# Products that nobody reads, issued on TensorE in five waits of a four-stage transformer kernel

## The chip, the cores and the metric

The kernel runs on one core of one Trainium2 chip. The metric is the device time of one execution in microseconds (us). TensorE is called PE, its weight loads PEld, VectorE DVE, ScalarE ACT, GpSimd POOL and SyncE SP, as in the rows of the profile.

## The reference

Two transformer layers over 2 x 1024 tokens of width 128, each an attention and a mixture of eight experts, each behind a layer norm and with a residual:

```python
x = x + _L0_attn_ref(_layernorm(x), ...)   # delta-rule attention, 4 heads, five branches, gates, fused, @ o_w
x = x + _L0_ffn_ref(_layernorm(x), ...)    # 8 experts, top 2, silu(x @ gate) * (x @ up) @ down
x = x + _L1_attn_ref(_layernorm(x), ...)   # 16 heads of width 8, rotary, softmax over 1024 keys, @ Wo + bo
x = x + _L1_ffn_ref(_layernorm(x), ...)    # 8 experts, top 1, gelu, @ Wo, layer norm
```

The end of the first attention, which the change touches, is

```python
fused = fused * jax.lax.rsqrt(jnp.mean(fused * fused, -1, keepdims=True) + 1e-05) * onorm_w
return fused.reshape(B, L, H * dv) @ o_w
```

## The kernel before

The 2048 tokens are 16 tiles of 128 (`NT`) in four blocks of 512 (`NB`). The four stages (`attn0`, `ffn0`, `attn1`, `ffn1`) run one behind the other, with `nc.all_engine_barrier()` between them (lines 2550 and 2557 are the first two). Each stage is one hand-written instruction stream for each engine; semaphores order them. At a barrier each engine has to have finished its own stream before any of them goes on.

The end of `attn0` on PE: for each block `j`, `mean_square(j)` (line 2390) sums the squares over the heads into a PSUM bank, ACT takes the root in two activations (lines 2097 and 2100, with a table load between them), DVE scales (line 1825), and `out(j)` (line 2397) multiplies by `o_w`. DVE adds that to `x` (line 1832) and takes the statistics of the next norm (lines 117 and 120). Some products of this stage are already ones that nobody reads: `hold(bank, times)`, line 2386, each 128 x 512 in bf16.

The head of `ffn0` and of `attn1`: DVE makes the roots (lines 127 and 129) and then 16 normalized tiles (`norm_rows`, line 135). PE turns them, four tiles a block (`norm_pe`, line 146), ACT copies each block to `xnT` (line 157). In `ffn0` PE then makes the router's logits (line 191), which DVE waits for at line 229, the first step of the routing. In `attn1` PE turns two blocks and then makes the projections of queries and keys, two products a block (lines 877 and 878), which DVE takes at lines 998 and 1000.

The end of `ffn0`: the expert loop ends on PE; ACT scales the rows that came back by DMA (line 612), and after each block increments `f0_scaled`, eight times in all (`2 * NB`). DVE adds and takes statistics.

Of the kernel before, what the change touches and what calls it, by code (L numbers as in the profile page):

```python
# [6 lines left out]
BF16 = mybir.dt.bfloat16  # L7
# [4 lines left out]
P = 128  # L12
# [4 lines left out]
BLK = 512  # L17
NB = T // BLK
# [120 lines left out]
def norm_pe(c, banks, blocks=range(NB)):  # L139
    pe, ps, k, xn, ident = c.pe, c.psum, c.turn, c.mem["xn"], c.mem["ident"]  # L140
    for b in blocks:
        pe.wait_ge(c.sem("n_row"), NT * k + TPB * (b + 1))
        if b >= len(banks):
            pe.wait_ge(c.sem("n_xnt"), NB * k + b - len(banks) + 1)
        for j in range(TPB):
            mm = pe.transpose(ps[:, banks[b % len(banks)], j * P:(j + 1) * P], xn[:, TPB * b + j, :], ident[:])
        mm.then_inc(c.sem("n_turned"), 1)
# [35 lines left out]
def logits_pe(c, name, weights):  # L183


    pe, ps, S = c.pe, c.psum, c.sem
    tokens = c.mem["xnT"][:, 0:T].rearrange("p (t q i) -> p t q i", q=4, i=32)
    for n in range(NB):
        pe.wait_ge(S("n_xnt"), NB * c.turn + n + 1)
        for q in range(4):  # L190
            mm = pe.matmul(ps[32 * q:32 * q + 32, 2, n * P:(n + 1) * P], weights, tokens[:, n * TPB:(n + 1) * TPB, q, :],
                           start=True, stop=True, skip_group_check=True)
    mm.then_inc(S(name + "_lgt"), 1)


def route_pe(c, name, top):
    pe, ps, s, S = c.pe, c.psum, c.mem, c.sem
    n, TC = width_of(top), top * NT
    pe.wait_ge(S(name + "_chosen"), 1)
    pe.wait_ge(c.own_pool.sem, c.filled)  # L200
    chosen = s["sel" if top == 2 else "first"][:].rearrange("p t e -> p (t e)")
    pe.matmul(ps[:, 3, 0:NT * NE], s["earlier"][:], chosen, start=True, stop=True)
    pe.matmul(ps[:, 4, 0:NT * NE], s["ones"][:], chosen, start=True, stop=True).then_inc(S(name + "_counted"), 1)
    step = 2 * TPB
    for q in range(0, TC, step):
        pe.wait_ge(S(name + "_lane"), q // step + 1)
        pe.wait_ge(S(name + "_carry"), q // step + 1)
        for k in range(q, q + step):
            mm = pe.matmul(ps[:, 5, 0:2 * n], s["at_lane"][:, k, :], s["carry"][:, k].rearrange("p c n -> p (c n)"),
                           start=k == 0, stop=k == TC - 1)  # L210
    mm.then_inc(S(name + "_found"), 1)
# [346 lines left out]
    return lambda b: c.mem["xnT"][:, b * BLK:(b + 1) * BLK]  # L558


def rows_out_sp(c, name, k, rows=NT):

    c.sp.wait_ge(c.sem("n_row"), NT * c.turn + rows)
    c.sp.dma_start(c.rows_x[k].rearrange("(p t) d -> p t d", p=P), c.mem["xn"][:]).then_inc(c.sem(name + "_rows"), 16)


def ffn0_sp(c, w):
    for name in ("up", "down"):
        c.sp.dma_start(c.mem["e_" + name][:], w["f0_" + name]).then_inc(c.sem("f0_weights"), 16)
    c.weights = 32  # L570
    rows_out_sp(c, "f0", 0)
    attn1_loads(c, w)
    results_sp(c, "f0", 2, c.rows_y[0])
# [18 lines left out]


def ffn0_pe(c):
    norm_pe(c, (6, 7))
    c.pe.wait_ge(c.sem("f0_tables"), c.tables)
    logits_pe(c, "f0", c.mem["f0_rw"][:])
    route_pe(c, "f0", 2)
    experts_pe(c, "f0", 2, True)


def ffn0_act(c):
# [14 lines left out]
def ffn0(c, w, x):  # L617
    ffn0_sp(c, w)
    ffn0_dve(c, x)
    ffn0_pe(c)  # L620
    ffn0_act(c)
    route_pool(c, "f0", 2)
    experts_pool(c, "f0", 2, c.rows_x[0], c.rows_y[0])
    attn1_ahead(c)
# [236 lines left out]
def attn1_pe(c):  # L861
    pe, ps, m, S = c.pe, c.psum, c.mem, c.sem
    xnT, q, kk, va, pt, o = m["xnT"], m["a1_q"], m["a1_k"], m["a1_va"], m["a1_p"], m["a1_o"]
    norm_pe(c, NORM_BANKS, (0, 1))
    pe.wait_ge(c.ahead.sem, c.ahead.n)

# [479 lines left out]
def attn1(c, w, x):  # L1346
    attn1_sp(c)
    attn1_pe(c)
    attn1_act(c, x)
    attn1_dve(c, x)  # L1350
    attn1_pool(c, x)
    tables_sp(c, w, "f1", 1)
# [769 lines left out]
def attn0_pe(c):  # L2122
# [108 lines left out]
    for n in range(NB):  # L2231
# [3 lines left out]
        for i, (_, g0, ng) in enumerate(FIRS):  # L2235
# [4 lines left out]
            for g in range(ng):  # L2240
                for h in range(H0):
                    mm = pe.matmul(ps[32 * h:32 * h + 32, fir_bank(n, i), :], m["a0_wfir"][:, (g0 + g) * H0 + h, :],  # L2242
                                   v4[:, h, b, PAD + t0 - 4 * g:PAD + t0 - 4 * g + BLK],
                                   start=g == 0, stop=g == ng - 1, skip_group_check=True)
# [80 lines left out]
    for n in range(NCH):  # L2325
        bank = SUO[n % 2]
        pe.wait_ge(S("a0_wn"), n + 1)
        for b in range(B):
            if n:
                pe.wait_ge(S("a0_sc"), (n - 1) * B + b + 1)  # L2330
            for hs in HEADS:
                mm = pe.matmul(ps[hs, bank[b], 0:3 * CH], st[hs, b, :], sbuf[hs, n % 2, b, :, :],
                               start=False, stop=False, skip_group_check=True)
# [3 lines left out]
        for b in range(B):  # L2337
            pe.wait_ge(S("a0_uh"), n * B + b + 1)
            so = ps[:, bank[b], 0:3 * CH].rearrange("p (o i) -> p o i", o=3)[:, 0:3:2, :]
            for hs in HEADS:  # L2340
                mm = pe.matmul(so[hs], uh[hs, b, :], op[hs, n, b, KTOK:AT + 1, :],
                               start=False, stop=True, skip_group_check=True)
# [45 lines left out]
    def mean_square(j):  # L2388
        pe.wait_ge(S("a0_fu2"), j + 1)
        pe.matmul(ps[:, MS[j], :], m["a0_heads"][:], sq[:, j % 2, :], start=True, stop=True).then_inc(S("a0_ms"), 1)  # L2390

    def out(j):
        pe.wait_ge(S("a0_scaled"), j + 1)
        pe.wait_ge(S("a0_mul"), min(NB * NU - 2 + j, NB * NU))
        for t in range(TPB):
            at = ORD[j] * BLK + t * P
            mm = pe.matmul(ps[:, OUT[j], t * D:(t + 1) * D], fu[:, at:at + P], m["a0_ow"][:], start=True, stop=True)
        mm.then_inc(S("a0_out"), 1)
# [33 lines left out]
    out(0)  # L2432
    mean_square(2)
    out(1)
    mean_square(3)
    out(2)
    out(3)


def attn0(c, w, x):  # L2440
# [144 lines left out]
```

## Time and profile before

| | |
|---|---|
| median of 3 runs | 923.98 us (923.12 to 925.49) |
| the profiled execution | 930.92 us, its span 929.6 us |
| mean granted PE clock | 0.898 |
| PE busy | 756.1 us, 81% of the span |
| DVE busy | 667.4 us, 72% |
| ACT busy | 511.1 us, 55% |

The span runs from the first to the last instruction. The stages lie at about 0 to 238, 238 to 422, 422 to 805 and 805 to 930 us of it. A granted clock of 1.00 is 2.4 GHz, one of 0.50 is 1.2 GHz; a value between them in a window says that the clock changed inside that window.

### The profile page before, as it was taken

Reading aid. Unit: us, or ns where it says so; the run is one execution under the profiler, and the core shown is the slowest. Engines: PE = TensorE matmul, PEld = TensorE weight load, DVE = VectorE, ACT = ScalarE, POOL = GpSimd, SP = SyncE. Lnnn points to the kernel's source line nnn. Section 1 sums busy time; section 2 is a strip of 40 time slices with the busy share of each in tenths; the row PEclk is TensorE's granted clock in tenths of the full one; section 3 lists DMA queues with packets and bytes.
Section 4 is the critical chain, followed back from the end, with each engine's and each line's share of the span. In section 5 each row is a group of like instructions: output and inputs, shape, how many; then the busy total and the mean of one; then the engine's idle time right before and its main releaser. Section 6 shows DMA issues by size and latency. Waiting matters only on the chain. (4 is left out here: it accounts for less than half of the span.)

```text
span 929.6 us, 17693 instructions
## 1 busy us (share of the span) xinstructions
PE 756.1 (81%) x6703; PEld 325.6 (35%) x6704; DVE 667.4 (72%) x1316; ACT 511.1 (55%) x1012; POOL 243.9 (26%) x297
## 2 busy tenths in 40 slices
PE   6999978967329999927887999999999999728880
PEld 2343256633216766714111222222222222215660
DVE  7868964477763344338786999999999998753545
ACT  4744413646203333344346888888888889704343
POOL 0130010323055666460651200000010000025653
PEclk9999979988659999977658999999999999958996
DMA  3520010000731111131876030312300000061113
GB/s 94 119 65 2 1 25 5 4 1 0 269 129 38 43 43 43 35 102 52 233 159 194 2 81 2 81 26 58 80 3 2 3 2 12 1 252 44 43 35 96
DMA packets 40618, 57.62 MB, mean 62 GB/s; under 512 B 12424, under 2 KB 27920, under 8 KB 39768
## 3 DMA queue, kind: packets, MB, share of 16 engines
q1 hardware_dynamic: 36568, 48.36, 19.1%
q0 software_dynamic: 3968, 8.13, 3.1%
q8 instruction: 55, 0.90, 0.4%
q14 instruction: 27, 0.22, 0.1%
HBM read 37.54 MB, written 14.75 MB: 56 GB/s over the span
## 5 line engine op out<-in xcount | busy, mean ns | idle before, releaser
L1019 DVE TENSOR_REDUCE arena<-psum 128x1 f32<-128x1024 f32 x256 | 301.0, 1217 | 23.5 <-PE psum L903 20.7
L1158 ACT ACTIVATE arena<-psum 128x512 f32<-128x512 f32 x512 | 265.9, 605 | 53.7 <-PE psum L922 53.6
L903 PE MATMUL psum<-arena 56*128 56x512 bf16 x512 | 181.0, 413 | 10.7 <-DVE arena L1019 9.1
L922 PE MATMUL psum<-arena 59*128 59x512 bf16 x512 | 156.3, 390 | 5.1 <-ACT arena L1158 3.7
L933 PE MATMUL psum<-arena 128*32 128x512 f32 x1024 | 138.4, 612 | 8.7 <-issue 8.7
L922 PEld LDWEIGHTS psum<-arena 59*128 59x128 bf16 x512 | 38.4, 94 | 165.8 <-ACT arena L1158 142.1
L475 POOL DMA_INDIRECT rows_y<-arena x62 | 61.9, 998 | 61.3 <-DVE arena L426 57.9
L383 PEld LDWEIGHTS psum<-arena 128*128 128x128 f32 x496 | 62.4, 191 | 37.9 <-issue 29.5
L383 PE MATMUL psum<-arena 128*128 (+1 forms) x496 | 66.9, 278 | 9.1 <-ACT arena L454 6.0
L374 PE MATMUL psum<-arena 128*128 x124 | 67.2, 625 | 3.5 <-DVE arena L411 2.7
L1227 POOL TENSOR_SCALAR arena<-arena 128x16 f32<-128x16 f32 x16 | 4.1, 254 | 249.5 <-DVE arena L1019 249.4
L470 POOL DMA_INDIRECT arena<-rows_x,arena x62 | 60.1, 969 | 35.4 <-issue 16.1
L903 PEld LDWEIGHTS psum<-arena 56*128 56x128 bf16 x512 | 37.5, 95 | 71.2 <-DVE arena L1019 69.0
L426 DVE COPY arena<-psum 128x128 f32<-128x128 f32 x62 | 18.1, 291 | 58.2 <-issue 36.3
L454 ACT COPY arena<-psum 128x512 f32<-128x512 f32 x62 | 36.2, 584 | 41.3 <-PE psum L389 37.9
L448 ACT ACTIVATE arena<-psum 128x512 f32<-128x512 f32 x39 | 23.3, 597 | 46.9 <-PE psum L374 46.9
L432 DVE TENSOR_TENSOR arena<-arena,psum 128x512 f32<-128x512 f32 x39 | 26.8, 688 | 23.5 <-PE psum L394 22.0
L2242 PE MATMUL psum<-arena 128*32 128x512 f32 x352 | 41.2, 593 | 0.2 <-DMA arena<-arena 0.2
L394 PE MATMUL psum<-arena 128*128 x78 | 40.8, 606 | 0.0
L389 PE MATMUL psum<-ident,arena 128*128 128x128 f32 x248 | 37.7, 275 | 0.0
L933 PEld LDWEIGHTS psum<-arena 128*32 128x32 f32 x1024 | 20.7, 108 | 42.4 <-issue 38.0
L418 DVE TENSOR_TENSOR arena<-psum,arena 128x512 f32<-128x512 f32 x23 | 15.9, 691 | 25.4 <-PE psum L374 19.5
(319 smaller groups left out, 1110.1 us busy)
## 6 DMA issues: line engine op xcount, KB each, us to landing
arena<-scr_k SPq DMA_DIRECT2D x15, 448.0 KB
arena<-scr_q SPq DMA_DIRECT2D x15, 448.0 KB
arena<-in_f_up SPq DMA_DIRECT2D x1, 4096.0 KB
arena<-rows_y SPq DMA_DIRECT2D x12, 256.0 KB, 4.5
scr_q<-arena SPq DMA_DIRECT2D x6, 384.0 KB, 3.7
arena<-in_f_down SPq DMA_DIRECT2D x1, 2048.0 KB
rows_x<-xn SPq DMA_DIRECT2D x2, 1024.0 KB, 16.8
arena<-in_f_up SPq DMA_DIRECT2D x1, 2048.0 KB, 8.4
```

What stands on the lines that cost most here:

```text
L374: pe.matmul(ps[:, u.pair, :], xt[:, u.pair, :], merged(wup[:, bass.ds(e, 1), 0:F]), start=True, stop=True).then_inc(up, 1)
L383: mm = pe.matmul(ps[:, 5 + 2 * d.pair, 0:P], ht[:, f * P:(f + 1) * P], merged(wdown[:, ed, f * P:(f + 1) * P]), start=f == 0, stop=f == FC ...
L389: mm = pe.transpose(ps[:, 4, f * P:(f + 1) * P], h[:, g.pair, f * P:(f + 1) * P], ident[:])
L394: pe.matmul(ps[:, 2 + u.pair, :], xt[:, u.pair, :], merged(wup[:, bass.ds(e, 1), F:2 * F]), start=True, stop=True).then_inc(again, 1)
L470: pool.indirect_dma_start(xs[:, t % SLOTS, :], None, src, index).then_inc(landed[t % SLOTS], 16)
L475: pool.indirect_dma_start(dst, index, y[:, d.slot, :], None).then_inc(stored[d.slot], 16)
L903: mm = pe.matmul(ps[:, bank + half, :], q[rows, k, h, (qh * 4 + qt) * P:(qh * 4 + qt + 1) * P], kk[rows, k, h, half * BLK:(half + 1) * BLK ...
L922: pe.matmul(ps[:, score_bank(n), :], kk[0:KA, k, h, kb * P:(kb + 1) * P], q[0:KA, k, h, qh * BLK:(qh + 1) * BLK], start=True, stop=True).t ...
L933: mm = pe.matmul(ps[32 * h:32 * h + 32, 7, :], va[:, kb, (st % NG) * HG + h, :], pt[:, (u % 3) * HG + h, :], start=kb == 0, stop=kb == NTB ...
L1019: dve.tensor_reduce(mx[:, qh, h * 4 + qt:h * 4 + qt + 1], ps[:, bank:bank + 2, :].rearrange("p a b -> p (a b)"), X, ALU.max).then_inc(S("a ...
L1158: act.activation(pt[:, (u % 3) * HG + h, :], ps[:, score_bank(n), :], ACT.Exp, scale=float(HD) ** -0.5).then_inc(S("a1_exp"), 1)
L2242: mm = pe.matmul(ps[32 * h:32 * h + 32, fir_bank(n, i), :], m["a0_wfir"][:, (g0 + g) * H0 + h, :], v4[:, h, b, PAD + t0 - 4 * g:PAD + t0 - ...
```

## The change

PE gets 35 more products of 128 x 512 in bf16, whose results nobody reads, at five places: six between `out(1)` and `mean_square(3)`, ten behind `out(3)` at the end of `attn0`, eight at the head of `ffn0` before the first transpose, six behind the expert loop of `ffn0` once ACT has scaled the last rows, five at the head of `attn1`. All but the first six use the identity matrix, read as bf16, and write PSUM bank 0; the first six write bank 1 by the function that stands there already.

```diff
+def idle_products(c, times):
+
+    bits = c.mem["ident"][:].bitcast(BF16)
+    for _ in range(times):
+        c.pe.matmul(c.psum[:, 0, :], bits[:, 0:P], bits[:, 0:1].broadcast_to([P, BLK]), start=True, stop=True)
...
 def ffn0_pe(c):
+    idle_products(c, 8)
     norm_pe(c, (6, 7))
     c.pe.wait_ge(c.sem("f0_tables"), c.tables)
     logits_pe(c, "f0", c.mem["f0_rw"][:])
     route_pe(c, "f0", 2)
     experts_pe(c, "f0", 2, True)
+    c.pe.wait_ge(c.sem("f0_scaled"), 2 * NB)
+    idle_products(c, 6)
...
 def attn1_pe(c):
...
+    idle_products(c, 5)
     norm_pe(c, NORM_BANKS, (0, 1))
...
     mean_square(2)
     out(1)
+    hold(1, 6)
     mean_square(3)
     out(2)
     out(3)
+    idle_products(c, 10)
```

On PE, where `attn0` ends and `ffn0` begins, the order before the change is this (L2397 is `out`, L2390 `mean_square`, L146 the transposes):

```order
L2390 MATMUL psum<-arena 128x512 [waits a0_fu2]
L2397 MATMUL psum<-arena 128x128 [waits a0_mul,a0_scaled]
L2397 MATMUL psum<-arena 128x128 x3
L2397 MATMUL psum<-arena 128x128 [waits a0_mul,a0_scaled]
L2397 MATMUL psum<-arena 128x128 x3
L146 MATMUL psum<-ident,xn 128x128 [waits barrier_Pool_Activation_PE_DVE_SP_release,n_row]
```

With the change the same place on PE reads as follows (L2397 is now the product of `hold`, L2401 `mean_square`, L2408 `out`, L565 the product of `idle_products`):

```order
L2397 MATMUL psum<-arena 128x512 x6
L2401 MATMUL psum<-arena 128x512 [waits a0_fu2]
L2408 MATMUL psum<-arena 128x128 [waits a0_mul,a0_scaled]
L2408 MATMUL psum<-arena 128x128 x3
L2408 MATMUL psum<-arena 128x128 [waits a0_mul,a0_scaled]
L2408 MATMUL psum<-arena 128x128 x3
L565 MATMUL psum<-ident 128x512 x10
L565 MATMUL psum<-ident 128x512 [waits barrier_Pool_Activation_PE_DVE_SP_release]
L565 MATMUL psum<-ident 128x512 x7
L146 MATMUL psum<-ident,xn 128x128 [waits n_row]
```

Six products now stand ahead of `mean_square(3)`, ten between `out(3)` and the barrier, and eight between the barrier and the first transpose; the barrier's release is waited for by the first of these eight.

Where `ffn0` ends and `attn1` begins, PE's order before the change is this (L383 is the last product of the experts, L877 and L878 the projections):

```order
L383 MATMUL psum<-arena 128x128
L146 MATMUL psum<-ident,xn 128x128 [waits barrier_Pool_Activation_PE_DVE_SP_release,n_row]
L146 MATMUL psum<-ident,xn 128x128 x3
L146 MATMUL psum<-ident,xn 128x128 [waits n_row]
L146 MATMUL psum<-ident,xn 128x128 x3
L877 MATMUL psum<-xnT,arena 128x512 [waits n_xnt,ahead]
```

With the change it is this (L888 is the first projection):

```order
L383 MATMUL psum<-arena 128x128
L565 MATMUL psum<-ident 128x512 [waits f0_scaled]
L565 MATMUL psum<-ident 128x512 x5
L565 MATMUL psum<-ident 128x512 [waits barrier_Pool_Activation_PE_DVE_SP_release]
L565 MATMUL psum<-ident 128x512 x4
L146 MATMUL psum<-ident,xn 128x128 [waits n_row]
L146 MATMUL psum<-ident,xn 128x128 x3
L146 MATMUL psum<-ident,xn 128x128 [waits n_row]
L146 MATMUL psum<-ident,xn 128x128 x3
L888 MATMUL psum<-xnT,arena 128x512 [waits n_xnt,ahead]
```

The six products of the stage's end wait for ACT's last scaled rows, and five more stand between the barrier and the transposes.

## Rows read from the trace of the kernel before

**Rows 1.** The page, part 2: granted clock in 40 slices, tenths.

```profile
PEclk9999979988659999977658999999999999958996
```

**Rows 2.** Windows of 1 us: engines' busy time, granted clock (third from last), DMA.

```profile
228.00:229.00 1.00, 0.52 (x1) 0.50 (x2) 0.96 (x8) 0.42 (x1) 0.00 (x0) 0.74 0.00 0
...
235.00:236.00 1.00, 0.14 (x2) 0.00 (x0) 0.96 (x8) 0.00 (x0) 0.00 (x0) 0.65 0.00 0
...
245.00:246.00 1.00, 0.86 (x20) 0.54 (x12) 0.06 (x1) 1.00 (x1) 0.00 (x0) 0.73 1.24 524
...
429.00:430.00 1.00, 1.00 (x3) 0.44 (x2) 0.00 (x0) 0.00 (x0) 0.00 (x0) 0.57 0.00 0
```

**Rows 3.** Timeline of PE: start us, us, what, [idle before <-releaser].

```profile
210.23 1.49 PE L2380 MATMUL psum<-arena 72*128 72x512 bf16 x3
211.51 0.63 PE L2386 MATMUL psum<-arena 128*128 128x512 bf16 x1
...
217.05 0.81 PE L2380 MATMUL psum<-arena 72*128 72x512 bf16 x3
217.69 0.38 PE L2386 MATMUL psum<-arena 128*128 128x512 bf16 x1
...
222.67 1.13 PE L2390 MATMUL psum<-arena 128*128 128x512 f32 x2 [0.70 <-ACT arena L2093]
223.64 1.05 PE L2397 MATMUL psum<-arena 128*128 128x128 f32 x8
228.48 2.08 PE L2390 MATMUL psum<-arena 128*128 128x512 f32 x2 [3.79 <-ACT arena L2093]
...
233.98 1.16 PE L2397 MATMUL psum<-arena 128*128 128x128 f32 x8 [1.83 <-DVE arena L1825]
239.98 4.19 PE L146 MATMUL psum<-ident,xn 128*128 128x128 f32 x16 [4.84 <-DVE xn L135]
244.10 1.76 PE L191 MATMUL psum<-xnT,arena 128*32 128x128 f32 x32
```

**Rows 4.** Timelines of ACT, then of DVE, from 224 to 247 us.

```profile
230.59 0.66 ACT L2097 ACTIVATE psum<-psum,arena 128x512 f32<-128x512 f32 x1 [2.17 <-PE psum L2390]
...
244.21 0.58 ACT L157 COPY xnT<-psum 128x512 f32<-128x512 f32 x1 [0.44 <-PE psum L146]
...
233.18 0.75 DVE L1825 SCALAR_TENSOR_TENSOR arena<-arena,psum 128x512 f32<-128x512 f32 x1 [2.20 <-ACT psum L2100]
...
235.76 0.65 DVE L1832 TENSOR_TENSOR x<-x,psum 128x512 f32<-128x512 f32 x1
...
238.06 0.17 DVE L127 TENSOR_SCALAR rs<-mv 128x16 f32<-128x16 f32 x1 [0.33 <-PEq L2550]
...
238.81 4.19 DVE L135 TENSOR_SCALAR xn<-x,mv,rs 128x128 f32<-128x128 f32 x16
...
245.94 0.72 DVE L229 STREAM_TRANSPOSE arena<-psum 128x512 f32<-128x512 f32 x1 [2.61 <-PE psum L191]
```

**Rows 5.** Timelines of PE, ACT and DVE from 398 to 434 us.

```profile
424.48 2.14 PE L146 MATMUL psum<-ident,xn 128*128 128x128 f32 x8 [21.68 <-DVE xn L135]
426.41 1.99 PE L877 MATMUL psum<-xnT,arena 128*128 128x512 f32 x2
428.20 1.86 PE L878 MATMUL psum<-xnT,arena 128*128 128x512 f32 x2
429.89 1.02 PE L877 MATMUL psum<-xnT,arena 128*128 128x512 f32 x2
...
409.81 9.45 ACT L612 ACTIVATE arena<-arena 128x128 f32<-128x128 f32 x32 [8.46 <-DMA arena<-rows_y]
...
422.56 0.18 DVE L127 TENSOR_SCALAR rs<-mv 128x16 f32<-128x16 f32 x1 [0.33 <-PEq L2557]
...
423.30 4.19 DVE L135 TENSOR_SCALAR xn<-x,mv,rs 128x128 f32<-128x128 f32 x16
430.17 0.75 DVE L998 SCALAR_TENSOR_TENSOR arena<-psum,arena 128x512 f32<-128x512 f32 x1 [2.68 <-PE psum L878]
```

## The prediction

> **What bounds the kernel now.** I read the granted clock first, since a product that nobody reads can only act through it or by being in the way. The page's clock row shows dips where one stage passes into the next [rows 1]. Windows of 1 us around those places then give the instants at which it changed: a window's value v between 0.5 and 1 means that the full clock (2.4 GHz, the other level being 1.2) was granted for (v - 0.5) / 0.5 of it. So it fell at 228.48 and again at 235.3, and rose at 245.54 and at 429.86 [rows 2]. Third, PE's timeline shows what the engine did around these: it idled 3.79 us before `mean_square(3)` and the clock fell just as that began; it idled 4.84 us before the transposes of `ffn0`, ran them and most of the logits at the low clock, and idled 21.68 us before those of `attn1`, where the clock rose 5.4 us after work began [rows 3, 5]. Fourth, the timelines of ACT and DVE say whether anybody waits for these slow products: ACT waits 2.17 us for `mean_square(3)`, DVE 2.61 us for the logits and 2.68 us for the first projection [rows 4, 5]. In all three the wait ends with PE, so PE's clock is on the path there. Behind the barriers all engines start together, so what is won before one is passed on.
>
> **What one added product costs.** A 128 x 512 bf16 product starts every 0.43 us at the low clock (three take from 210.23 to 211.51) and every 0.21 us at the full one (217.05 to 217.69) [rows 3]. All 35 are 15.1 us or 7.5 us of PE work, and all of it is put where PE idles; the cost is only what sticks out of each wait.
>
> **Six ahead of `mean_square(3)`.** They start when `out(1)` ends at 224.69, take 1.3 us and leave some 2.5 us of the 3.79 us idle, so nothing is late. If the clock holds, `mean_square(3)` takes 1.13 instead of 2.08 us [rows 3]; ACT, DVE line 1825 and `out(3)` follow from it one after another, so 0.95 us is the most. The least is nothing: 1.3 us of work in a wait of 3.79 us is thin. The clock fell at 235.3 too, where PE had idled 1.83 us and then worked 1.16 us [rows 2, 3], which is as thin. The instant of a change isn't tied to the work (one fall came just as work began, the other 0.16 us after it had ended), so executions will differ. I take **-0.4 us**, a little under the middle.
>
> **Ten behind `out(3)`.** PE ends its stage at 235.14; DVE, last at the barrier, ends at 238.06 - 0.33 = 237.73 [rows 3, 4]. So there are 2.6 us of cover. Ten products take 2.1 us at the full clock: free. At the low clock they take 4.3 us: the barrier comes 1.7 us later, and with it SP's loads, POOL, ACT and DVE's norm, which all stand behind it. The clock fell at 235.3, just as they would begin [rows 2]; with PE now at work from 233.98 on without a break it may hold, or come back partway. If it falls and stays low, 1.7 us are lost. Bounds 0 and +1.7; I take **+0.7 us**.
>
> **Eight at the head of `ffn0`.** The first four rows are ready 1.9 us behind the barrier's release (transposes at 239.98, DVE's first step at 238.06) [rows 3, 4]. Eight products take 1.7 us at the full clock, 3.4 us at the low one. After ten products and nearly without a pause I expect the full clock by then: PE would have worked since 233.98, and both rises in these rows came within 5.6 us of the start of work (239.98 to 245.54, 424.48 to 429.86) [rows 2, 3, 5]. What is gained: DVE ends its rows at 243.00 and gets the logits at 245.94, 2.94 us later [rows 4]. In that stand the last four transposes (a quarter of 4.19 us, 1.05, but paced by DVE's rows), a copy of 0.58 us on ACT, and the last quarter of the logits, from 244.79 to 245.86. At the full clock the transposes' work halves (-0.45) and the last logits too (-0.5): 0.95 us at most. In an execution where the clock rises earlier in this stretch than at 245.54 there is less to gain, so I take **-0.7 us**. If the products still ran at the low clock the transposes would begin 1.5 us late; that is the rival below.
>
> **Six at the end of `ffn0`.** They start with ACT's end at 409.81 + 9.45 = 419.26. At the low clock they take 2.6 us, to 421.9 or 422.0; DVE, again last at the barrier, ends at 422.56 - 0.33 = 422.23 [rows 5]. Cost nothing, covered by 0.2 us; without that cover (one product more) +0.2.
>
> **Five at the head of `attn1`.** From about 422.5, at the low clock, 2.1 us: to 424.7, where the first transpose stood at 424.48: +0.2 us on the transposes, +0 at the full clock. The gain: PE is now at work from 419.3 with a pause of 0.5 us instead of from 424.48. Before, the first projection's four products took from 426.41 to 430.06, DVE began at 430.17, and the clock rose at 429.86, too late for it [rows 2, 5]. At the full clock two of these take 1.02 instead of 1.99 us, so four take 1.75 instead of 3.5, and DVE starts at 428.4: **1.75 us** for a rise before 426.5. Were the clock up before the transposes too, they would end with DVE's rows of the second block (423.30 + 2.1 = 425.4) and half a us later the projection would start at 426.0: 2.3 us. The least is nothing. DVE then works on without a wait, so its start is what counts. With the 0.2 us against it, and some executions in which the clock rose earlier before the change than in this one, I take **-1.4 us**.
>
> The Trainium skill, page "TensorE: Matmul & The Clock Gate", section "Part 4: PE-mode transpose", speaks against this last term: it says that a transpose doesn't count as PE at work for the clock. By it the transposes would be a pause, and the clock would come only with the projections, as before: 0 instead of -1.4, the sum -0.4. The trace disagrees: at 245.54 the clock rose with PE at work since 239.98, 4.19 us of it in transposes and 1.4 us in logits [rows 2, 3].
>
> **The sum.** -0.4 + 0.7 - 0.7 + 0 - 1.4 = **-1.8 us**, 930.92 to 929.1 us in the profiled execution, where the low clock lay at unlucky instants and up to -3.7 us is possible. That execution is 6.9 us above the median of the runs; no row says where those lie, and I take the same difference off the median: 923.98 - 1.8 = **922.2 us**, 0.2% less. 0.3% (2.8 us) is about what this measurement can tell from no change.
>
> **The rivals.**
> *All of it works.* The clock holds in every wait: -0.95 + 0 - 0.95 + 0 - 2.3 = -4.2, 919.8 us. For it: PE's pauses shrink from 3.8 and 4.8 us to about 2.5 and under 1. Against: the fall at 235.3 after 1.16 us of work. Chance 0.23.
> *Transposes count as a pause* (worked out above from the rows: no gain at `attn1`), or the clock changes where it changed before: -0.4 to 0, 923.6 us. For it: 21.68 us of idleness before `attn1` end in products, not in a longer wait. Chance 0.17.
> *The low clock holds through the products between the two stages*, slower than before. Place: `out(3)` to the first transpose. The ten cost 1.7 us at the barrier and the eight end 1.5 us behind the first rows, so 3.2 us, less what PE catches up, plus 0.2 at `attn1`: +3.2, 927.2 us. It decides from the point at which the clock is low for more than about 6 of the 18 products (2.6 us of cover less 2.1 us leaves 0.5 us, two products, at the barrier; the gain of 0.7 us pays for three or four more). For it: the fall at 235.3. Against: PE works 6 us on end there, and no stretch of such work in the rows stayed at the low clock. Chance 0.12.
> *The forecast*, between these: -0.8 to -2.8 us, 922.2 us, chance 0.48.
>
> **How the numbers follow.** Faster by over 0.3%: all of "all works" and a tenth of the forecast, 0.28. Slower by over 0.3%: most of the slow rival, 0.10. Within: 0.62. The three runs of before spread over 2.4 us, so I set the range 1 us beyond the likeliest cases: 919.0 to 925.5; that leaves out the slow rival and the far end of the fast one.
>
> **What would show it.** Right: the granted clock near 1.00 from about 238 us to the logits (fell at 235.3 before), DVE line 229 under 2.5 us behind DVE's last row (2.94 before), and DVE's first step of `attn1` (line 998 before) within 5.6 us of the barrier's release (7.6 before). Wrong: a DVE wait ended by PE's sequencer at the first barrier of over 0.4 us (0.33 before), which is the ten products sticking out; the same at the second barrier; or a first transpose later than 2.0 us behind the release. The forecast is wrong if later stages answer to the earlier start otherwise than by moving up, as where `attn1` waits for its DMAs.

## The result, and the profile after

The changed kernel takes **928.02 us** (median of 9 runs, 922.86 to 933.48), the kernel before, run beside it, 922.98 us (9 runs, 921.52 to 925.49): ratio 1.0062, with a 95% interval of 1.0041 to 1.0082. It is slower by 0.6%, some 5 us, where 1.8 us less was forecast.

The head of the page of the changed kernel's profile, the clock row of part 2 and PE's instruction queue in part 3:

```profile
span 926.7 us, 17761 instructions
...
PE 759.9 (82%) x6736; PEld 328.5 (35%) x6739; DVE 667.1 (72%) x1316; ACT 511.5 (55%) x1012; POOL 243.9 (26%) x297
...
PEclk9999989987859999977758999999999999966995
...
q8 instruction: 55, 0.90, 0.4%
```

At the ninth to the twelfth slice the clock row reads 8785, where [rows 1] has 8865: the dip at the head of `ffn0` is shallower (8 instead of 6 in the eleventh slice), and the one at `attn1` is nearly as before (77758 instead of 77658). So the products act roughly as meant; the loss must lie elsewhere.

**Where the products stand.** PE's timeline of the changed kernel (columns as in [rows 3]); L2397 is the hold of six (one of the six has no record in this trace), L565 the ten and the eight, L2401 `mean_square`, L2408 `out`, L146 the transposes, L191 the logits:

```profile
226.86 1.25 PE L2397 MATMUL psum<-arena 128*128 128x512 bf16 x5
...
229.87 1.13 PE L2401 MATMUL psum<-arena 128*128 128x512 f32 x2 [1.75 <-ACT arena L2104]
...
234.42 1.16 PE L2408 MATMUL psum<-arena 128*128 128x128 f32 x8 [2.54 <-DVE arena L1836]
235.42 2.34 PE L565 MATMUL psum<-ident 128*128 128x512 bf16 x10
238.50 1.90 PE L565 MATMUL psum<-ident 128*128 128x512 bf16 x8 [0.75 <-PEq L2563]
240.42 0.66 PE L146 MATMUL psum<-ident,xn 128*128 128x128 f32 x4
...
244.08 1.17 PE L191 MATMUL psum<-xnT,arena 128*32 128x128 f32 x32
```

`mean_square(3)` took 1.13 us instead of 2.08, the ten ran in 2.34 us at the full clock, and the transposes and the logits too. DVE's timeline, at the two barriers and behind them (L127 is its first step there, L1009 what was L998):

```profile
238.50 0.17 DVE L127 TENSOR_SCALAR rs<-mv 128x16 f32<-128x16 f32 x1 [0.33 <-PEq L2563]
...
245.32 0.72 DVE L229 STREAM_TRANSPOSE arena<-psum 128x512 f32<-128x512 f32 x1 [1.55 <-PE psum L191]
...
422.42 0.17 DVE L127 TENSOR_SCALAR rs<-mv 128x16 f32<-128x16 f32 x1 [0.70 <-PEq L2570]
...
429.22 0.75 DVE L1009 SCALAR_TENSOR_TENSOR arena<-psum,arena 128x512 f32<-128x512 f32 x1 [1.86 <-PE psum L889]
```

From the barrier to the logits' first reader it is 6.82 us (245.32 - 238.50); before it was 7.88 (245.94 - 238.06, [rows 4]). From the next barrier to the first projection's reader it is 6.80 us, before 7.61 [rows 5]. The two stretches together are 1.9 us shorter; 0.4 us of it was lost again at the second barrier (see the six products of `ffn0`'s end, below). Up to here nothing has made the kernel slower.

**Where the time went.** The groups of the page put it into one row of the loop of `attn1`, the scores: keys times queries, where three of the 59 rows are the row maxima. The row of the page before, and the one after (busy, mean ns of one, idle before, who ended most of it):

```profile
L922 PE MATMUL psum<-arena 59*128 59x512 bf16 x512 | 156.3, 390 | 5.1 <-ACT arena L1158 3.7
```

```profile
L933 PE MATMUL psum<-arena 59*128 59x512 bf16 x512 | 156.4, 390 | 14.7 <-DMA arena<-scr_m 5.1
```

The work is the same, the idleness before it 9.6 us more, and a third of the row's idleness ends with a load that the row before doesn't name: `arena<-scr_m`. This is the turn of the small row maxima. Once in each of 16 rounds SP stores them with four DMAs of 3 KB (`scr_m<-arena`), waits for all four, and loads them back in another layout. SP's timeline before, three rounds:

```profile
639.50 1.71 SPq L1295 DMA_DIRECT2D scr_m<-arena  x4
642.24 0.71 SPq L1297 DMA_DIRECT2D arena<-scr_m  x1
...
679.18 1.71 SPq L1295 DMA_DIRECT2D scr_m<-arena  x4
681.90 0.70 SPq L1297 DMA_DIRECT2D arena<-scr_m  x1
...
775.25 1.71 SPq L1295 DMA_DIRECT2D scr_m<-arena  x4
777.99 0.70 SPq L1297 DMA_DIRECT2D arena<-scr_m  x1
```

and after:

```profile
638.18 1.71 SPq L1306 DMA_DIRECT2D scr_m<-arena  x4
643.22 0.71 SPq L1308 DMA_DIRECT2D arena<-scr_m  x1
...
681.44 1.71 SPq L1306 DMA_DIRECT2D scr_m<-arena  x4
686.07 0.70 SPq L1308 DMA_DIRECT2D arena<-scr_m  x1
...
781.63 1.72 SPq L1306 DMA_DIRECT2D scr_m<-arena  x4
784.38 0.70 SPq L1308 DMA_DIRECT2D arena<-scr_m  x1
```

The load is issued 2.7 us behind the first store before the change, and 5.0 and 4.6 us behind it after, in two of the rounds shown; so it is in six of the last eight rounds (from 638 us on), and not in the last one. (In the round from 723 us on it is on time too, at 2.7 us.) From DVE's L127 of `attn1` to the last of these loads it is 777.99 - 422.56 = 355.43 us before and 784.38 - 422.42 = 361.96 after: 6.5 us more. At 638 us the changed kernel was still 1.2 us ahead (638.18 - 422.42 against 639.50 - 422.56); from there to the last store it takes 143.45 instead of 135.75 us, 7.7 more.

**What is in the way of the stores.** The DMA view of the changed kernel from 641.1 to 642.5 us, in slices of 0.035 us (the row GB/s, the packets, and by queue: packets, MB, share of the engines):

```profile
GB/s 0 0 0 468 0 0 0 0 0 0 0 0 0 0 0 0 0 0 0 0 0 0 0 0 0 0 0 0 0 0 4 2 0 0 0 0 0 0 0 0
DMA packets 5, 0.02 MB, mean 12 GB/s; under 512 B 4, under 2 KB 4, under 8 KB 4
...
q8 instruction: 1, 0.02, 4.3%
q1 hardware_dynamic: 4, 0.00, 0.4%
```

One packet of the queue `q8 instruction` is under way, 16 KB and 0.96 us in the packet's own record (from 641.22), and four small packets of the last store come only as it ends, at 642.17; that store's other packets had ended at 640.56. In all late rounds of this kernel but the one from 763 us on it is just four packets that come behind the instruction packet. SP's wait is for all of them. PE then has nothing for its next unit (PE's timeline: 643.47, idle, 645.60), and the clock, which had been 1.00, falls for some 3 us (windows of 1 us, columns as in [rows 2]):

```profile
643.47 0.38 PE L933 MATMUL psum<-arena 59*128 59x512 bf16 x1
...
645.60 0.37 PE L933 MATMUL psum<-arena 59*128 59x512 bf16 x1 [1.75 <-issue]
```

```profile
644.00:645.00 1.00, 0.00 (x0) 0.00 (x0) 1.00 (x1) 0.76 (x2) 0.00 (x0) 1.00 0.04 12
...
646.00:647.00 1.00, 1.00 (x10) 0.16 (x8) 0.74 (x1) 0.99 (x2) 0.00 (x0) 0.72 0.00 0
647.00:648.00 1.00, 1.00 (x6) 0.13 (x4) 0.48 (x1) 0.10 (x1) 0.00 (x0) 0.50 0.00 0
```

What the packet carries is the instructions themselves. 55 packets of 16 KB are 0.90 MB; in the loop one comes about every 20 us, once in a round. Measured from the round's first store, it came 7.2 us behind it in the second half of the loop before the change, when the stores were long over, and comes 2.3 to 3.0 us behind it after, in all of these rounds but the last. That is read off the packet records of both traces. The distance alone does not settle it, though: of two rounds with the packet 2.5 and 2.6 us behind the store, one is late and one isn't, while the round with 3.0 us is late.

**What a late round costs.** From the third round on it is 19.84 us from a round's first store to the next one's, before the change and after, wherever the load is on time (16.72 to the last). Late rounds take 20.7 to 20.9 us (17.95 where it was 16.72), except the first of them, which takes 22.5 us (638.18 to 660.68). The fall of the clock in that round is a part of it, but not what makes the loss: of all later profiles with late rounds not one has a low clock from 506 us to the end of the loop. In the profile of e1_pad35, an experiment told below, PE idles even longer in one round (1.81 us), that round takes 21.4 us (682.43 to 703.83), and the clock stays up (PE's timeline, and the whole loop as one window):

```profile
689.92 0.37 PE L931 MATMUL psum<-arena 59*128 59x512 bf16 x1 [1.81 <-issue]
```

```profile
506.00:787.00 281.00, 257.06 (x1761) 59.00 (x1758) 259.58 (x238) 235.60 (x457) 22.69 (x75) 1.00 0.15 32
```

The profiled execution of before took 930.92 us and isn't one of the nine runs; after the last of these loads it needs 151.6 us to the end (929.6 - 777.99), the changed kernel 142.3. All later profiles of experiments whose "before" had a median of 934 us show 151 to 155 us there, and all with one of 923 us 142 to 143, whatever the kernel. So what comes behind the loop goes with the chip of the measurement, and the spans of profiles from two chips aren't compared below; stretches and ratios are.

### The profile page after: what moved, and what is told of

Read it like the earlier page. It is cut to its first block and busy times, and to the rows that moved or that the text cites. A ratio compares the mean times of both kernels' runs of the same rounds, so it can differ in the third digit from the quotient of the medians.

```text
span 926.7 us, 17761 instructions
## 1 busy us (share of the span) xinstructions
PE 759.9 (82%) x6736; PEld 328.5 (35%) x6739; DVE 667.1 (72%) x1316; ACT 511.5 (55%) x1012; POOL 243.9 (26%) x297
## 5 line engine op out<-in xcount | busy, mean ns | idle before, releaser
L914 PE MATMUL psum<-arena 56*128 56x512 bf16 x512 | 177.8, 411 | 11.8 <-DVE arena L1030 10.1
L383 PEld LDWEIGHTS psum<-arena 128*128 128x128 f32 x496 | 62.4, 191 | 29.5 <-issue 27.0
L383 PE MATMUL psum<-arena 128*128 (+1 forms) x496 | 66.3, 277 | 2.4 <-ACT arena L454 2.4
L944 PEld LDWEIGHTS psum<-arena 128*32 128x32 f32 x1024 | 20.7, 108 | 43.4 <-issue 39.4
```

The costliest lines, as they stand in the source:

```text
L383: mm = pe.matmul(ps[:, 5 + 2 * d.pair, 0:P], ht[:, f * P:(f + 1) * P], merged(wdown[:, ed, f * P:(f + 1) * P]), start=f == 0, stop=f == FC ...
L914: mm = pe.matmul(ps[:, bank + half, :], q[rows, k, h, (qh * 4 + qt) * P:(qh * 4 + qt + 1) * P], kk[rows, k, h, half * BLK:(half + 1) * BLK ...
L944: mm = pe.matmul(ps[32 * h:32 * h + 32, 7, :], va[:, kb, (st % NG) * HG + h, :], pt[:, (u % 3) * HG + h, :], start=kb == 0, stop=kb == NTB ...
```

## The experiments

**Theory A.** The 35 products with their weight loads are 70 instructions (the page counts 6704 weight loads before and 6739 after; of the products a few records are missing). They shift PE's stream against the packets that bring it, by 70 of 256 places if a packet holds 256; in the loop of `attn1` the packet then falls into the maxima's stores. **Rival B.** The stage begins in another state of clocks and arrival times, and the loop answers to that; the stream is innocent. **Rival C**, the prediction's slow one: the products stick out at the barriers.

All ratios are against the kernel before on the same chip, 12 runs of each experiment unless said, and 17 to 35 of before. "Late" are the maxima's loads issued over 4 us behind the first store (the first two rounds, where the first is late before too, aside). "Distance" is that of the instruction packet behind the first store in the second half of the loop, "loop" the stretch defined above.

| kernel | instructions added ahead of the loop | ratio [95%] | late | distance us | loop us |
|---|---|---|---|---|---|
| before | 0 | | 0 | 7.2 | 355.43 |
| changed | 70 | 1.0062 [1.0041, 1.0082] | 6 | 2.4 | 361.96 |
| e1_pad35 (6 runs) | 70 | 1.0079 [1.0061, 1.0098] | 7 | 2.4 | 362.36 |
| e2_pad128 | 256 | 1.0008 [0.9990, 1.0027] | 0 | 7.2 | 355.03 |
| e3_after_pad93 | 256 | 0.9978 [0.9963, 0.9993] | 0 | 7.2 | 353.35 |
| e4_pad17 | 34 | 1.0004 [0.9986, 1.0021] | 0 | 6.3 | 355.74 |
| e5_front_pad104 | 256 | 1.0015 [0.9992, 1.0037] | 0 | 7.3 | 353.89 |
| e6_second_pad117 | 256 | 0.9988 [0.9964, 1.0012] | 0 | 7.3 | 352.05 |
| e7_pad35_late | 0 (70 behind it) | 1.0000 [0.9977, 1.0023] | 0 | 7.3 | 355.90 |
| e8_few17 | 34 | 0.9995 [0.9970, 1.0021] | 0 | 6.3 | 353.68 |
| e9_pad45 (6 runs) | 90 | 1.0078 [1.0055, 1.0101] | 7 | 2.2, then 0.1 | 362.61 |
| e10_pad64 | 128 | 1.0007 [0.9989, 1.0025] | 0 | -2.3 | 356.27 |
| e11_changed_again | 70 | 1.0051 [1.0030, 1.0072] | 7 | 2.4 | 360.75 |
| e12_tail6_pad97 | 256 | **0.9966 [0.9944, 0.9987]** | 0 | 7.3 | 353.19 |

### The instructions without the places

The kernel before, with products of one column behind the expert loop of `ffn0`, where PE then idles for over 10 us. None of the five places of the change is touched. 35 of them take 1.03 us.

```diff
+def pad_products(c, times):
+    c.pe.wait_ge(c.sem("f0_ready"), tiles_of(2))
+    bits = c.mem["ident"][:].bitcast(BF16)
+    for _ in range(times):
+        c.pe.matmul(c.psum[:, 0, 0:1], bits[:, 0:P], bits[:, 0:1], start=True, stop=True)
...
     experts_pe(c, "f0", 2, True)
+    pad_products(c, 35)
```

**e1_pad35**: 35 such products.

> The kernel before, with 35 products of 128 x 1 (zeros, read by nobody) on PE behind the expert loop of the first expert layer, where PE idles for some 17 us in any case. They add as many instructions to PE's stream as the change does, but next to no work for the array, and none of it in the waits that the change fills. Theory A (the length of the stream: PE's instructions come in by 16 KB packets of DMA queue 8, 0.96 us each, and the added instructions move these packets onto the small stores and loads of the row maxima, L1306 and L1308 of the changed kernel, in the second attention's loop): slower by 3 to 6 us, like the change, with 2 to 5 of the 16 loads of maxima issued over 4.5 us behind their stores (2.7 us where nothing is in the way). Theory B (the added products harm by their work: the barrier, the clock, an earlier start of the second attention): same as before, within 0.15%.

**e2_pad128**: 128 instead, so 256 instructions, which put the stream back to where it was if a packet holds 256.

> The kernel before, with 128 products of 128 x 1 at the same place. Each is a weight load and a product, 256 instructions of 64 bytes, just one packet of 16 KB. Theory A: the packets after it fall where they fell before, so the same as before within 0.15%. Theory A' (what counts is how many instructions there are, not where packets fall): slower, and by more than with 35. Theory B: the same.

**e4_pad17**: 17.

> The kernel before, with 17 products of 128 x 1 at the same place: half the shift. In the profile of before the packets of queue 8 come 7.1 us behind the stores of the maxima, in that of the changed kernel 2.4 us. By theory A half the shift puts them at about 4.8 us, behind the loads, so the same as before within 0.2% or up to 1 us slower where it reaches the loads' packets. Theory A' (more instructions cost more): slower by half of what 35 cost. Theory B: the same.

e1_pad35 is slower by 0.8%: 941.85 us against 934.63. All that the changed kernel loses is there, with none of its products in its place, and more than I had expected (7.2 us against 3 to 6, seven late loads against two to five). The loop alone is 6.9 us longer than in the profile of before (362.36 to 355.43). More than three times as many instructions, e2_pad128, cost nothing (+0.1%, within the interval). The waits of SP's queue from 600 to 780 us (total us, times, longest) show the difference, e1_pad35 and then e2_pad128:

```profile
SPq L1306 <- DMA scr_m<-arena: 22.2, 9, 3.3
```

```profile
SPq L1306 <- DMA scr_m<-arena: 9.1, 9, 1.0
```

A wait has a longest of 1.0 us where the packet is elsewhere and of 3.3 us where it is in the way. The page of e2_pad128 has one packet more, for 256 instructions more:

```profile
q8 instruction: 56, 0.92, 0.4%
```

That fits 256 to a packet but does not prove it, since e10_pad64 below has 56 packets as well, with 128 more. What does speak for 256 is the distance, which is back at 7.2 us with 256 more and at no other number tried.

The Trainium skill says so as well (page "Runtime: NRT & Kernel Launch", section "Instruction fetch mechanics"): an engine's instructions are refilled in blocks of 16 KiB, 256 instructions, by a DMA queue that its sequencer drives. It adds that crossing a block is mostly hidden. What the block's own transfer does to other transfers that section doesn't say; here a load went out 2.3 us later in one round (5.0 instead of 2.7 us behind the first store). e4_pad17 did no harm, as expected, but the distance was 6.3 us and not the 4.8 that I had worked out in proportion: the packet does not move evenly with the instructions.

### The change with its stream put back

**e3_after_pad93**: the changed kernel, and 93 products of one column behind the expert loop of `ffn0` (35 + 93 = 128).

```diff
     experts_pe(c, "f0", 2, True)
+    pad_products(c, 93)
     c.pe.wait_ge(c.sem("f0_scaled"), 2 * NB)
     idle_products(c, 6)
```

> The changed kernel, with 93 products of 128 x 1 behind the expert loop of the first expert layer, ahead of the six: with the 35 of the change they make 256 instructions. Theory A: the second attention is as before the change, and what is left is what the 35 products win: 1 to 2 us under before, 5 to 7 us under the changed kernel. Theory B: as the changed kernel, about 5 us over before.

0.9978, faster by 0.2% with an interval that leaves out 1. All five places are as in the changed kernel, and what differs is the stream (and PE at work for some 3 us more of its long wait in `ffn0`, which e2_pad128 has too, without a gain): this decides against B. It decides against C too: in this execution the ten products did stick out (below), and the kernel is still 0.8% faster relative to before than the changed one (0.9978 to 1.0062). SP's waits from 600 to 780 us are those of before again:

```profile
SPq L1317 <- DMA scr_m<-arena: 10.1, 10, 1.0
```

**e7_pad35_late**: the kernel before with the 35 (without the wait in front) in `ffn1`, between its logits and its routing, behind the loop of `attn1`.

```diff
     logits_pe(c, "f1", c.mem["f1_rw"][:])
+    pad_products(c, 35)
     route_pe(c, "f1", 1)
```

> The kernel before with 35 products of 128 x 1 only in the last stage, between the logits and the routing of the second expert layer, where PE idles. Theory A: the packets of PE's instructions in the second attention lie as before, so same as before, within 0.15%. Theory A' (70 more instructions anywhere cost 5 to 7 us): slower by 0.6 to 0.8%.

Ratio 1.0000 [0.9977, 1.0023]. The program is as long as that of e1_pad35, so its length as such isn't what costs; 70 instructions cost nothing that can be measured where no small store hangs on the packets that follow.

### How it goes with the number

**e9_pad45** and **e10_pad64**: as e1_pad35, with 45 and 64 products.

> The kernel before with 45 products of 128 x 1 behind the first expert layer's expert loop, ten more than the 35 that cost 0.8%. In the second half of the second attention's loop the packets of PE's instructions then come some 0.8 us earlier than with 35: nominally 0.2 us behind the first store of the maxima instead of 1.8 us, so that they are through before the stores' last packets. Theory A: no late loads in that half, some in the first half, where the distance still drifts; slower than before by 0 to 4 us, less than with 35 (7 us). Theory A' (more instructions cost more): slower than with 35, 9 us.

> The kernel before with 64 products of 128 x 1 at that place, 128 instructions, half a packet. Nominally the packets come 2.8 us ahead of the stores in the second half of the loop. Theory A: no late loads there; 0 to 2 us slower than before, from rounds that are met in passing in the first half. Theory A': 13 us slower.

17, 35, 45, 64, 128 products: nothing that can be told, +0.8%, +0.8%, nothing, nothing. A cost by number is excluded; one by position is what is seen. But the expectation for 45 was a miss, by the size: I had it below e1_pad35, and it is the same. Its seven late loads are in the first half of the loop; in the second the distance drifts from 1.4 to 0.1 us and the load is 3.4 to 3.9 us behind the store. SP's waits of e9_pad45 from 480 to 600 us, and those of the changed kernel there:

```profile
SPq L1306 <- DMA scr_m<-arena: 13.8, 5, 3.0
```

```profile
SPq L1308 <- DMA scr_m<-arena: 5.6, 5, 1.6
```

So the harmful position is some 2 to 3 us behind the first store, about where the last of the four is under way, and which rounds get there differs from kernel to kernel: all late rounds of these profiles, from the third on, have the packet 2.1 to 3.0 us behind. Not all rounds with such a packet are late; the one at 2.55 us in the changed kernel, one at 2.8 in e1_pad35 and one at 2.95 in e11_changed_again are on time. A small delay is free: in e9_pad45 two rounds with the load at 3.5 and 3.6 us take 19.84 us as before, those at 3.8 to 3.9 us 20.1 to 20.25, those at 4.3 to 4.6 us 20.6 to 20.9. This is why e10_pad64, with loads at 3.2 to 3.8 us in six rounds, costs next to nothing.

**e8_few17**: the changed kernel without the ten and the eight: 17 products, 34 instructions. The edit against the changed kernel:

```diff
 def ffn0_pe(c):
-    idle_products(c, 8)
     norm_pe(c, (6, 7))
...
     out(3)
-    idle_products(c, 10)
```

> The changed kernel without the ten and the eight: six ahead of the last mean square, six at the end of the first expert layer, five at the head of the second attention, 17 in all, and nothing added to fill a packet. They are as many instructions as the 17 products of 128 x 1, which cost nothing that could be measured. Theory A: faster than before by 1 to 2.5 us (-0.4 and -1.4 of the prediction's terms). Theory A' (the number of instructions counts) or B: slower by 1 us or more.

No late loads, 0.9995 [0.9970, 1.0021]: the change without its loss. The gain of 1 to 2.5 us that I expected isn't shown, nor excluded.

### The places, with the stream kept whole

**e5_front_pad104**: only the first three places (6, 10, 8), and 104 products of one column. **e6_second_pad117**: only the last two (6, 5), and 117. The edits against the changed kernel, in this order:

```diff
-    c.pe.wait_ge(c.sem("f0_scaled"), 2 * NB)
-    idle_products(c, 6)
+    pad_products(c, 104)
...
-    idle_products(c, 5)
     norm_pe(c, NORM_BANKS, (0, 1))
```

```diff
-    idle_products(c, 8)
     norm_pe(c, (6, 7))
...
+    pad_products(c, 117)
...
-    hold(1, 6)
...
-    idle_products(c, 10)
```

> The kernel before with only the first three of the five places (six ahead of the last mean square, ten behind the last output of the first attention, eight at the head of the first expert layer), and 104 products of 128 x 1 behind that layer's expert loop, so that from there on PE's stream is longer by 256 instructions, one packet. Theory A: nothing happens in the second attention's loop, and what is measured is the front alone, by the prediction's terms -0.4 + 0.7 - 0.7 = -0.4 us: between 1.5 us under and 0.7 us over before. Theory B (the front's products harm the barrier): 1 to 3 us slower.

> The kernel before with only the last two places (six at the end of the first expert layer, five at the head of the second attention), and 117 products of 128 x 1 behind the expert loop: again 256 instructions. Theory A: the prediction's last term alone, -1.4 us, between -0.5 and -2.3. Theory B (an earlier start of the second attention's head meets its DMAs): slower by 1 us or more.

1.0015 and 0.9988, both with 1 inside: no part by itself can be told from nothing by its time, and for the front, where I expected 1.5 us under to 0.7 us over, the value is 1.4 us over, with an interval from 0.7 us under to 3.5 over. Their stretches can be read: behind the first barrier e5_front_pad104 needs 6.82 us to the logits' reader, as the changed kernel; behind the second e6_second_pad117 needs 5.43 us to the projection's, where before took 7.61.

**e11_changed_again**: the changed kernel once more, on another chip.

> The changed kernel itself, once more, beside the kernel before on the same chip as these two. Every theory: slower than before by 0.4 to 0.8%, as measured. Theory A adds that its profile shows loads of the maxima over 4.4 us behind their stores in the second half of the second attention's loop, with the packets 2.3 to 3.0 us behind the stores, as in its first profile; if the harm were a chance of that one execution, they would be at 2.7 us.

1.0051, the same loss, and seven late loads where the first profile had six. Its profile also shows what the first one did not. PE's and DVE's timeline:

```profile
227.50 2.07 PE L2401 MATMUL psum<-arena 128*128 128x512 f32 x2 [2.48 <-ACT arena L2104]
...
233.99 4.01 PE L565 MATMUL psum<-ident 128*128 128x512 bf16 x10
...
238.30 0.17 DVE L127 TENSOR_SCALAR rs<-mv 128x16 f32<-128x16 f32 x1 [1.55 <-PEq L2563]
```

Here the hold held nothing (2.07 us), the ten ran at the low clock, and DVE waited 1.55 us at the barrier instead of 0.33.

**e12_tail6_pad97**: the changed kernel with six instead of ten behind `out(3)`, and 97 of one column to make 128 in all.

```diff
     out(3)
-    idle_products(c, 10)
+    idle_products(c, 6)
...
     experts_pe(c, "f0", 2, True)
+    pad_products(c, 97)
```

> A version meant to beat both kernels: the changed kernel with six instead of ten products behind the last output of the first attention, and 97 products of 128 x 1 behind the first expert layer's expert loop, so that the 31 and the 97 make 256 instructions. In two profiles with ten products DVE's wait at the first barrier was 0.95 and 1.55 us instead of 0.33 us; six take 2.6 us at the low clock and fit. Theory A: no late loads of maxima in the second attention's loop, 1.5 to 3 us under before (with ten products and 93 it was 0.22%, 2.1 us, under). If the six are too few to bring the clock up for the head of the expert layer, the stretch from DVE's line 127 to its transpose is 7.9 us instead of 6.8, and the gain is 1 us.

918.84 us against 922.59, 0.9966 [0.9944, 0.9987]: faster than before by 0.3%, and by their ratios faster than the changed kernel too (1.0062 and 1.0051, on other chips). Its timelines of PE and DVE:

```profile
234.35 2.47 PE L565 MATMUL psum<-ident 128*128 128x512 bf16 x6
...
237.44 0.17 DVE L127 TENSOR_SCALAR rs<-mv 128x16 f32<-128x16 f32 x1 [0.33 <-PEq L2572]
...
420.84 0.17 DVE L127 TENSOR_SCALAR rs<-mv 128x16 f32<-128x16 f32 x1 [0.50 <-PEq L2579]
...
426.27 0.75 DVE L1018 SCALAR_TENSOR_TENSOR arena<-psum,arena 128x512 f32<-128x512 f32 x1 [0.50 <-PE psum L898]
```

Six products at the low clock take 2.47 us and end within the cover of 2.6 us that DVE gives.

## Why the prediction was wrong

**The step that failed** is in "What one added product costs": "All 35 are 15.1 us or 7.5 us of PE work, and all of it is put where PE idles; the cost is only what sticks out of each wait." The time that the products take was rightly counted; that they are also 70 instructions of PE's stream was not. What the runs showed in its place: the 70 instructions alone, elsewhere, cost 7.2 us (e1_pad35), and with 186 more instructions to make a whole packet the change gains 2.3 us (e3_after_pad93, 932.31 against 934.63 us). The forecast for all five places, -1.8 us, was thus near what they give without that shift, and the loss of 5 us is their gain of some 2 us and a cost of some 7 us, which begins 215 us behind the last barrier that I had looked at. That the gain is as forecast is known only roughly: the interval of e3_after_pad93 reaches from 0.7 to 3.5 us.

**"DVE then works on without a wait, so its start is what counts"** fell with it. The start of `attn1` did move, by 0.8 us from the barrier, and at 638 us the kernel was still 1.2 us ahead. The prediction ended by saying that it fails "if later stages answer to the earlier start otherwise than by moving up, as where `attn1` waits for its DMAs". They do wait for a DMA, but for another reason than the earlier start: e3_after_pad93 starts at least as early, and none of its loads is late.

**The slow rival** gave 927.2 us, close to the measured 928.02, by a mechanism that isn't what made the loss. In the changed kernel's first profile the ten ran at the full clock, and in e11_changed_again, where they ran low and cost 1.2 us at the barrier, the eight ran at the full clock all the same (1.90 us); in neither did the first transpose come late. That its number is near the measured one is luck.

**Term by term**, over the profiles that have the product in question:

- *Six ahead of `mean_square(3)`*, forecast -0.4 within 0 and -0.95. In the six profiles with the hold `mean_square(3)` took 1.13 us three times (the changed kernel, e5_front_pad104, e8_few17), 1.26 once (e3_after_pad93) and 2.07 or 2.08 twice (e11_changed_again, e12_tail6_pad97); in the eight without it 1.77 to 2.08, never less. The three good ones are those in which the clock had fallen early, with `mean_square(2)` at 1.95 to 2.06 us. Where it had fallen as early without the hold (e4_pad17, e7_pad35_late, e9_pad45, e10_pad64), `mean_square(3)` took 1.77 to 1.98, so those gains are the hold's. Against the row's 2.08 us the mean is some -0.6, against the eight's mean -0.5: right, a little small.
- *Ten behind `out(3)`*, forecast +0.7 within 0 and +1.7. DVE's wait at the barrier grew by 0, 0.6 (0.95 us in e3_after_pad93) and 1.2 us (1.55 in e11_changed_again). Right in kind and size, and e12_tail6_pad97 took the term away by fitting the number to the cover.
- *Eight at the head of `ffn0`*, forecast -0.7, at most -0.95. It was -1.06 us in all five profiles with the eight (6.81 or 6.82 us from barrier to reader, against 7.88), also where the ten ran low; without them 7.83 to 8.04, but for e8_few17 with 6.99, where the clock happened to rise just ahead of the logits. Right in kind, and beyond the bound that I gave: the last transposes end 5.65 instead of 6.11 us behind the barrier, the 0.45 that I took, but the logits then take 1.17 instead of 1.76 us, 0.6 and not 0.5.
- *Six at the end of `ffn0`*, forecast nothing. They took 2.34 us and ended at 421.70, with DVE's last step (421.72). Right; but DVE waited 0.70 us instead of 0.33 at this barrier, for POOL, whose drain at the barrier ended last, at 422.13 (before it ended at 422.06, ahead of DVE's at 422.28). Of what was won before it 0.4 us was lost there. That barriers pass on what is won was too simple: this one passes on only what all engines have won.
- *Five at the head of `attn1`*, forecast -1.4 within 0 and -2.3. It was -0.8 in the changed kernel, where the clock rose at 428.0, and -2.2 in e3_after_pad93, e6_second_pad117, e11_changed_again and e12_tail6_pad97 (in the second it rose at 424.73, with DVE's L127, before the transposes), with -2.05 in e8_few17. Before's 7.61 us isn't typical, though: the eight profiles without the five have 6.51 to 7.67, mean 7.3, and the 6.80 of the changed kernel lies among them. The six with the five have a mean of 5.7, 1.6 us less. The sign that I had set, within 5.6 us of the barrier's release, is missed in the changed kernel's first profile and met in the other five. Right, and a little low.

The clock and the transposes: in e8_few17 PE idled 4.84 us before the transposes of `ffn0`, then did nothing else from 241.73 to the logits at 245.56, and the clock rose at 245.2. PE's timeline and windows there:

```profile
241.73 3.90 PE L146 MATMUL psum<-ident,xn 128*128 128x128 f32 x16 [4.84 <-DVE xn L135]
```

```profile
244.00:245.00 1.00, 1.00 (x5) 0.69 (x5) 1.00 (x6) 0.56 (x2) 0.00 (x0) 0.50 1.22 524
245.00:246.00 1.00, 1.00 (x20) 0.84 (x23) 0.07 (x1) 0.85 (x2) 0.26 (x2) 0.90 0.93 393
```

The rule of the Trainium skill (page "TensorE: Matmul & The Clock Gate", section "Part 4: PE-mode transpose") that a transpose doesn't count as PE at work is not borne out by this trace: here the clock rose with nothing but transposes behind the idleness, while the rise at 245.54 that the prediction went by had 1.4 us of logits in front of it. And the rival that hung on it (no gain at `attn1`) did not come about in five of the six profiles with the five products.

**What stays open.** Why the packet's distance is 7.2, 6.3, 2.4 and -2.3 us for 0, 34, 70 and 128 added instructions, and drifts with 90, was not settled: when PE's sequencer asks for a packet is in no view. Nor is it shown why four packets of a store wait for the instruction packet at all (in the first late round they are missing already 0.7 us before that packet's own record begins, 640.56 to 641.22), or why the load then goes out 4.3 to 5.0 us behind the first store and not 2.7 + 0.96. How much of the 7.7 us the clock took can be estimated: the same round with the clock up, in e11_changed_again, takes 21.2 instead of 22.5 us, so some 1.3 us is the clock's and the rest the lateness itself. Why the clock fell there and not in e1_pad35 after a longer idleness is open.

## What to carry to other kernels

An instruction added where its engine idles still costs bytes in the stream of that engine, and moved the later fetches here by a fraction of a packet; if a round of a loop has a small transfer on its path, look in the trace at what the instruction queue does beside it. Before a change that adds or removes instructions is judged, run the old kernel with the same number of idle ones (e1_pad35), and the new one filled up to a whole packet of 256 (e3_after_pad93); the two together part what the work does from what its position does. And fit products that keep the clock up to the cover at the barrier by their time at the low clock, since in some executions that is what they get.

## What the runs showed of the hardware

- A packet of the instruction queue is 16 KB and takes 0.9 to 1.5 us by its own record in the changed kernel's profile (0.96 in the round read above), and four packets of a 3 KB store of the same core came 1.6 us behind their siblings (642.17 against 640.56) when one was in the way. The load that waited for them was issued 4.3 to 5.0 us behind the first store instead of 2.7.
- 70 more instructions ahead of the loop cost 0.8% (e1_pad35), 256 more nothing that can be told (1.0008 [0.9990, 1.0027]), nor 128 more, nor 70 more behind the loop: what counts in this kernel is where the fetches fall, and not how many instructions there are.
- PE's idleness of 1.75 us, in a loop that had been at the full clock from 503 us on, was followed within 1 us of its end by a low clock of 3.4 us (646.44 to 649.85); one of 1.81 us in e1_pad35 was not. Nor does the clock change at the same places in two executions of one kernel: in the changed kernel's two profiles it rose 5.6 and 0.5 us behind the second barrier (427.98 - 422.42, 422.02 - 421.55).
- The clock rose behind 4.84 us of idleness with PE at nothing but transposes (e8_few17: transposes from 241.73, rise at 245.2, logits from 245.56).
- 35 products of one column take 1.03 us in all, 29 ns each with their weight loads.
